# Expert tiles of a graph and mixture-of-experts layer: gathered rows scaled, shifted and split by rows, then turned by transposing DMAs in place of TensorE transposes

## The chip, the cores and the metric

One Trainium2 chip, one core. The metric is the device time of one execution in microseconds (us), the median of several runs. Engines: PE is TensorE, DVE is VectorE, ACT is ScalarE, POOL is GpSimd, SP is SyncE, which here only issues DMAs.

## The reference, cut to what matters

6250 nodes of 256 features pass a graph attention layer and a linear attention layer, which take up the first two thirds of the time and stay as they are. What the change touches is the last layer, a mixture of eight experts of which each node uses two:

```python
logits = xt @ Wr + br                       # xt: the normalized nodes, 6250 x 256
top_p, top_idx = top_k(softmax(logits), 2)
weights = top_p / top_p.sum(-1)
xn = (xt - mu) * rsqrt(var + 1e-5)
xe = xn * ln_g[e] + ln_b[e]                 # scale and shift of expert e, one number per feature
h  = gelu(xe @ W1[e] + b1[e])               # 256 -> 1024
y  = h @ W2[e] + b2[e]                      # 1024 -> 256
out = x + sum over the two experts of weights * y
```

## The kernel before, in words

Until about 1350 us into the span the kernel does the two attention layers, the routing and a sort of the nodes by expert. It ends with a table `places`: for each of FT = 56 tiles of 256 places (two halves of 128, called sub), which node stands in each place, and with `ffn_i`, the expert of each tile. The normalized rows lie in DRAM in `xn2_d` (the trace calls it xn_d).

Each tile s then runs through all engines, with two buffers (u = s % 2) for nearly everything:

- **POOL** (`pool_turn`, L877) makes one turn for each i from 0 to 60, in program order: it waits until a rows buffer is free (`rows_turned`, L880), until the result of tile i - 5 is weighted (`y_gated`) and until both adds of tile i - 6 have landed (`y_added`); it copies the turn's places (`places_now`, L857); issues the first half's indirect add of tile i - 5 into the output in DRAM (`add_rows`, L862); two indirect gathers of weights for tile i - 3 (`get_gates`, L867); waits until the first add has landed; issues the second add (L862); and at last two indirect gathers of 128 rows of 256 float32 for tile i (`get_rows`, L873) into `rows_s[u]`. Turns 0 to 4 add nothing, turns past 55 gather no rows.
- **PE** (`pe_tile`) turns the rows of tile s + 1 with four float32 transposes into PSUM (`pe_turn_rows`, L2219), so that the features lie on the partitions; does 48 matmuls of tile s against W1 (`pe_up`, L2233); and 48 matmuls of tile s - 1 against W2 (`pe_down`, L2253). Values and weights are each split in a high and a low float16 part, three products of them are summed, hence 48.
- **DVE** (`dve_tile`) makes `dve_affine(s + 1)`: two TENSOR_SCALARs read the turned rows from PSUM, multiply and add the expert's scale and shift, which here are one number per partition (L1880, into `x_f`), wait for ACT's high part, and subtract it to get the low part (L1885). Then it splits the activations of tile s (L1900, L1901), four times 512 columns, and forms y of tile s - 1 from PSUM (`dve_answer`, L1914).
- **ACT** (`act_tile`) rounds `x_f` of tile s + 1 to float16 (`act_high`, L1166), makes the gelu of tile s from PSUM (L1145) and weights y of tile s - 1 (`act_gate`, L1158).
- **SP** has nothing to do in this stage: its last DMAs are the weights W2 and the store of the gates (L728), and then it waits for the end (L732).

The scales and shifts of all experts come in at the start with b1 and bq: four small loads on ACT's queue into `param_rows`, one transpose on PE, a copy and a small multiply on DVE (L1277, L1279). Wr and br have a semaphore of their own (`route_in`); POOL waits for the seven other parameter loads before it adjusts a bias (L775, L776).

The order of the stage is fixed by each engine's program order and semaphores:

```python
def pe_tile(b, u):
    s = b * 2 + u
    if not (isinstance(s, int) and s + 1 == FT):
        pe_turn_rows(s + 1, 1 - u, b + u)
    pe_up(s, u)
    ...
        pe_down(s - 1, 1 - u)
```

Of the kernel before, what the change touches and what calls it, by code (L numbers as in the profile page):

```python
# [9 lines left out]
P = 128  # L10
# [26 lines left out]
FR = 2 * P  # L37
# [103 lines left out]
def build(nc, x, src, dst, gnn_w, attn_l, attn_r, gnn_bias, wq, bq, wk, bk, wv, bv, wo, bo,  # L141
          wr, br, ln_g, ln_b, w1, b1, w2, b2, out):
    ctx = ExitStack()
    with ctx:
# [51 lines left out]
        param_rows = first([98, P])  # L196
# [84 lines left out]
        params = sb("params", [P, 98])  # L281
        b1T, gT, bT, bqT = params[:, 0:64], params[:, 64:80], params[:, 80:96], params[:, 96:98]
# [47 lines left out]
        params_s = params[:, 64:96]  # L330
# [28 lines left out]
        x_f = ffn([P, 2, KD, FR])  # L359
# [77 lines left out]
        def high_hots_of(t0, t1):  # L437
# [39 lines left out]
        route_in, blank_turn = sem("route_in"), sem("blank_turn")  # L477
# [22 lines left out]
        place_turn, table_turn, map_turn, places_ready = sem("place_turn"), sem("table_turn"), sem("map_turn"), sem("places_ready")  # L500
        now_ready = sem("now_ready")
        adds_ready, tau_turn = sem("adds_ready"), sem("tau_turn")
        rows_got = [sem(f"rows_got{u}") for u in range(2)]
        gates_got = [sem(f"gates_got{u}") for u in range(2)]
        rows_turned, x_turn, x_high, h_made, gelu_ready, h_turn, y_made, y_ready, y_gated, y_added = (
            sem("rows_turned"), sem("x_turn"), sem("x_high"), sem("h_made"), sem("gelu_ready"), sem("h_turn"),
# [38 lines left out]
        def _(sp):  # L545
# [17 lines left out]
            def load_mix(n):  # L563
                if n < 2:
                    sp.dma_start(w_kv[:, :, n, :], (wk, wv)[n].rearrange("(k p) n -> p k n", p=P)).then_inc(mix_in, 16)
                elif n < 4:
                    sp.dma_start(b_kv[:, n - 2, :], (bk, bv)[n - 2].rearrange("(a n) -> a n", a=1).to_broadcast([P, D])).then_inc(mix_in, 16)
                elif n < 6:
                    sp.dma_start((w_q, w_o)[n - 4][:, :, :], (wq, wo)[n - 4].rearrange("(k p) n -> p k n", p=P)).then_inc(mix_in, 16)
                elif n == 6:  # L570
                    sp.dma_start(bo_b[:, :], bo.rearrange("(a n) -> a n", a=1).to_broadcast([P, D])).then_inc(mix_in, 16)
                elif n == 7:
                    sp.dma_start(wr_s[:, :, :], wr.rearrange("(k p) n -> p k n", p=P)).then_inc(route_in, 16)
                else:
                    sp.dma_start(br_b[:, :], br.rearrange("(a n) -> a n", a=1).to_broadcast([P, X])).then_inc(route_in, 16)
# [150 lines left out]
            load_w2(7)  # L726
            sp.wait_ge(gates_ready, 1)
            sp.dma_start(gate_d.rearrange("(p t) e -> p t e", t=T), gates[:, :, :]).then_inc(gates_out, 16)  # L728

            for g in range(GROUPS - 2, GROUPS):  # L730
                sp.wait_ge(x2_out[g % 2], x2_stored(g))
# [4 lines left out]
        def _(pool):  # L736
# [38 lines left out]
            pool.wait_ge(mix_in, 7 * 16)  # L775
# [142 lines left out]
        def _(act):  # L918
# [3 lines left out]
            act.dma_start(param_rows[64:80, :], ln_g.rearrange("e (f p) -> (e f) p", p=P)).then_inc(params_in, 16)  # L922
            act.dma_start(param_rows[80:96, :], ln_b.rearrange("e (f p) -> (e f) p", p=P)).then_inc(params_in, 16)
            act.dma_start(param_rows[96:98, :], bq.rearrange("(f p) -> f p", p=P)).then_inc(params_in, 16)
# [210 lines left out]
            def act_tile(b, u):  # L1135
                s = b * 2 + u
                if not (isinstance(s, int) and s + 1 == FT):
                    act_high(s + 1, 1 - u)
# [30 lines left out]
            act_high(0, 0)  # L1169
# [12 lines left out]
        def _(dve):  # L1182
# [92 lines left out]
            def keep_params():  # L1275
                dve.wait_ge(params_turned, 1)
                dve.tensor_copy(params[:, :], bank[7][:, 0:98]).then_inc(params_kept, 1)  # L1277
                dve.wait_ge(params_kept, 1)
                dve.tensor_scalar(params_s[:, :], params[:, 64:96], ASCALE, None, ALU.mult).then_inc(params_kept, 1)  # L1279
# [553 lines left out]
            in_turn(dve, map_turn, 0,  # L1833
# [8 lines left out]
            dve.wait_ge(map_turn, 7)  # L1842
# [4 lines left out]
            in_turn(dve, map_turn, 7,  # L1847
# [6 lines left out]
            dve.wait_ge(map_turn, 13)  # L1854
            dve.sem_inc(adds_ready, 1)

            def find_adds():

                dve.wait_ge(unused_placed, 1)
                in_turn(dve, tau_turn, 0,  # L1860
# [9 lines left out]
                dve.wait_ge(tau_turn, 9)  # L1870
# [15 lines left out]

            def dve_tile(b, u):
                s = b * 2 + u
                if not (isinstance(s, int) and s + 1 == FT):
                    e1 = dve.value_load(ffn_i[0:1, bass.ds(s + 1, 1)], min_val=0, max_val=X - 1)  # L1890
                    dve_affine(s + 1, 1 - u, e1)
# [26 lines left out]
            dve.wait_ge(params_kept, 2)  # L1918
            dve.wait_ge(b2_in, 16)
            dve_affine(0, 0, dve.value_load(ffn_i[0:1, 0:1], min_val=0, max_val=X - 1))  # L1920
# [12 lines left out]
        def _(pe):  # L1933
# [7 lines left out]
            def turn_params():  # L1941
                pe.wait_ge(params_in, 4 * 16)
                pe.transpose(bank[7][:, 0:98], param_rows[:, :], ident[0:98, 0:98]).then_inc(params_turned, 1)
# [179 lines left out]
            def keys_hook(b, u):  # L2123
# [4 lines left out]
                if u == 1:  # L2128
                    if not later:
                        pe.wait_ge(mix_in, 7 * 16)  # L2130
# [38 lines left out]
            pe.wait_ge(route_in, 32)  # L2169
# [43 lines left out]
            def pe_turn_rows(s, u, b):  # L2213
                pe.wait_ge(rows_got[u], (b + 1) * 32)
                if not (isinstance(s, int) and s < 2):
                    pe.wait_ge(x_turn, 2 * s - 3)
                for k in range(KD):
                    for sub in range(2):
                        last = pe.transpose(bank[6 + u][:, k * FR + sub * P:k * FR + (sub + 1) * P],  # L2219
                                            rows_s[:, u, sub, k * P:(k + 1) * P], ident[:, :])  # L2220
                last.then_inc(rows_turned, 1)
# [18 lines left out]
            def pe_down(s, u):  # L2240
                if isinstance(s, int) and s == 0:
                    pe.wait_ge(w2_in, X * 16)
                    pe.wait_ge(tau_turn, 1)
# [32 lines left out]
            pe_turn_rows(0, 0, 0)  # L2276
# [37 lines left out]
```

## Time and profile before

| | |
|---|---|
| median of 3 runs | 1996.78 us (1994.44 to 1999.62) |
| the profiled execution, own time | 1998.07 us |
| its span in the profile | 1996.4 us |
| PE busy | 1659.0 us, 83% |
| DVE busy | 1503.7 us, 75% |
| POOL busy | 1325.6 us, 66% |
| ACT busy | 854.8 us, 43% |
| bytes moved by DMA | 238.93 MB, mean 120 GB/s |
| expert stage (first row gather to the end) | about 1357 to 1996 us |

The span is that of one profiled execution; its own time is 1.7 us longer than the span, and 1.3 us above the median. Times of single instructions below are in that span. "Idle before" is what an engine waited just before an instruction, with what released it.

### The profile page before, as it was taken

Reading aid. Unit: us, or ns where it says so; the run is one execution under the profiler, and the core shown is the slowest. Engines: PE = TensorE matmul, PEld = TensorE weight load, DVE = VectorE, ACT = ScalarE, POOL = GpSimd, SP = SyncE. Lnnn points to the kernel's source line nnn. Section 1 sums busy time; section 2 is a strip of 40 time slices with the busy share of each in tenths; the row PEclk is TensorE's granted clock in tenths of the full one; section 3 lists DMA queues with packets and bytes.
Section 4 is the critical chain, followed back from the end, with each engine's and each line's share of the span. In section 5 each row is a group of like instructions: output and inputs, shape, how many; then the busy total and the mean of one; then the engine's idle time right before and its main releaser. Section 6 shows DMA issues by size and latency. Waiting matters only on the chain.

```text
span 1996.4 us, 48372 instructions
## 1 busy us (share of the span) xinstructions
PE 1659.0 (83%) x11492; PEld 1334.3 (67%) x11493; DVE 1503.7 (75%) x4295; ACT 854.8 (43%) x2066; POOL 1325.6 (66%) x1235
## 2 busy tenths in 40 slices
PE   7767777777787788888887675947999999999996
PEld 5545455555556677666765454936888998988885
DVE  6667677878777888888889888988666666666663
ACT  4633344444433444444444443583444434344442
POOL 2077777777777777677767774404777777777774
PEclk8979999999999999999999988557999999999998
DMA  7745556565534554444444553851333333333342
GB/s 218 231 122 144 161 148 172 151 175 159 135 110 113 141 141 128 132 138 135 127 119 131 155 193 106 301 196 35 54 51 46 51 47 52 49 47 51 46 51 28
DMA packets 150531, 238.93 MB, mean 120 GB/s; under 512 B 27984, under 2 KB 116168, under 8 KB 149192
## 3 DMA queue, kind: packets, MB, share of 16 engines
q0 software_dynamic: 62784, 134.26, 30.2%
q1 hardware_dynamic: 85944, 103.15, 15.6%
q10 hardware_dynamic: 1744, 0.85, 0.2%
q8 instruction: 23, 0.38, 0.1%
q14 instruction: 36, 0.29, 0.0%
HBM read 181.73 MB, written 56.44 MB: 119 GB/s over the span
## 4 chain that ended last, share of the span: by engine, by line
PE 31%; issue 19%; DVE 18%; POOL 18%; DVEq 6%; DMA 6%; POOLq 1%; ACT 0%; SPq 0%; ACTq 0%
POOL w_s L805 16%; PE bank L2233 13%; PE bank L2253 13%; DVE w_s L1501 5%; DMA w_s<-table,w_s 3%; DVEq L1436 3%; DMA out<-mid_g,acc 2%; PE bank L2219 1%; DVE w_s L1491 1%; PE bank L2046 1%; DVE w_s L1487 1%; DVE w_s L1484 1%; DMA w_s<-in_x 1%; DVE acc L1512 1%; DVE acc L1664 1%
## 5 line engine op out<-in xcount | busy, mean ns | idle before, releaser
L805 POOL DMA_INDIRECT w_s<-table,w_s x784 | 840.3, 1072 | 281.8 <-issue 235.3
L2046 PE MATMUL bank<-w_s 128*128 128x260 f32 x1952 | 513.3, 409 | 93.7 <-DVE w_s L1501 91.9
L2046 PEld LDWEIGHTS bank<-w_s 128*128 128x128 f32 x1952 | 375.0, 199 | 194.5 <-DVE w_s L1501 118.7
L1501 DVE SCALAR_TENSOR_TENSOR w_s<-w_s 128x256 f32<-128x256 f32 x976 | 347.7, 417 | 0.0
L1001 ACT COPY w_s<-bank 128x512 bf16<-128x512 bf16 x244 | 143.6, 588 | 409.0 <-PE bank L2026 314.3
L2233 PE MATMUL bank<-acc,w_s 128*128 128x256 f16 x2688 | 303.8, 273 | 0.0
L2253 PE MATMUL bank<-w_s,acc 128*128 x2688 | 302.6, 273 | 1.0 <-DVE acc L1914 1.0
L2253 PEld LDWEIGHTS bank<-w_s,acc 128*128 128x128 f16 x2688 | 262.7, 98 | 32.0 <-issue 1.3
L2233 PEld LDWEIGHTS bank<-acc,w_s 128*128 x2688 | 263.4, 98 | 30.8 <-issue 0.2
L862 POOL DMA_INDIRECT out<-mid_g,acc x112 | 196.4, 1753 | 80.7 <-POOL acc L857 47.0
L1468 DVE SCALAR_TENSOR_TENSOR w_s<-w_s,iota 128x512 bf16<-128x512 f32 x244 | 182.9, 749 | 6.7 <-issue 1.4
L1158 ACT ACTIVATE mid_g<-acc 128x256 f32<-128x256 f32 x112 | 50.8, 500 | 304.2 <-DMA out<-mid_g,acc 154.5
L1145 ACT ACTIVATE acc<-bank,params 128x256 f32<-128x256 f32 x448 | 172.7, 480 | 18.7 <-issue 14.8
L1901 DVE SCALAR_TENSOR_TENSOR acc<-acc 128x512 f16<-128x512 f32 x224 | 157.6, 704 | 7.7
L995 ACT ACTIVATE w_s<-w_s 128x16 f32<-128x16 f32 x244 | 56.4, 231 | 233.6 <-DVE w_s L1493 230.3
L989 ACT CAST w_s<-w_s 128x512 f32<-128x512 bf16 x244 | 152.5, 625 | 0.0
L2026 PEld LDWEIGHTS bank<-w_s 128*128 128x128 bf16 x976 | 68.1, 101 | 117.5 <-DVE w_s L1468 69.0
L2036 PE MATMUL bank<-w_s 128*128 x976 | 63.6, 176 | 99.7 <-DVE w_s L1489 51.7
L867 POOL DMA_INDIRECT acc<-gate_d,acc x112 | 117.6, 1050 | 35.2 <-issue 33.6
L2026 PE MATMUL bank<-w_s 128*128 128x128 bf16 x976 | 99.8, 227 | 47.8 <-DVE w_s L1468 46.9
L873 POOL DMA_INDIRECT acc<-xn_d,acc x112 | 111.1, 992 | 35.6 <-issue 26.2
L1914 DVE SCALAR_TENSOR_TENSOR acc<-bank,stage 128x256 f32<-128x256 f32 x112 | 42.3, 419 | 120.2 <-PE bank L2253 120.1
(301 smaller groups left out, 2226.5 us busy)
## 6 DMA issues: line engine op xcount, KB each, us to landing
stage<-in_L_ffn_W SPq DMA_DIRECT2D x32, 512.0 KB, 3.3
w_s<-table,w_s POOLq DMA_INDIRECT x784
w_s<-in_x SPq DMA_DIRECT2D x48, 256.0 KB, 4.2
w_s<-xT_d SPq DMA_DIRECT2D x96, 128.0 KB
w_park<-low_g SPq DMA_DIRECT2D x18, 512.0 KB
w_s<-w_park SPq DMA_DIRECT2D x9, 1024.0 KB, 9.2
xn_d<-acc SPq DMA_DIRECT2D x7, 896.0 KB, 4.7
table<-w_s SPq DMA_DIRECT2D x24, 260.0 KB, 3.6
```

Source lines behind the costliest of these rows:

```text
L805: pool.indirect_dma_start(out=ring[:, u, k, :], out_offset=None, in_=table[:, :], in_offset=bass.IndirectOffsetOnAxis(ap=ids[:, h, at + u, ...
L862: pool.indirect_dma_start(out=out[:, :], out_offset=bass.IndirectOffsetOnAxis(ap=now[:, h, sub:sub + 1], axis=0), in_=gated_s[:, 1 - h, su ...
L989: act.copy(hot32[:, k.at % 4, :, :], hot16[:, k.at % 4, :, :]).then_inc(hot32_ready, 1)
L1001: act.copy(hotT[:, k.at % 2, :, :], turned16).then_inc(hotT_ready, 1)
L1145: last = act.activation(h32[:, f, :], bank[q][:, (f % 2) * FR:(f % 2 + 1) * FR], ACT.Gelu, bias=b1T[:, bass.ds(e * KF + f, 1)], scale=UNSCALE)
L1468: dve.scalar_tensor_tensor(hot16[:, k.at % 4, :, :], dstT[:, bass.ds(group * SUB, SUB)].unsqueeze(2).to_broadcast([P, SUB, P]), tile_v[:, ...
L1501: last = dve.scalar_tensor_tensor(m[:, e:e + GH, 0:GD], rows[:, e:e + GH, 0:GD], 1.0, m[:, e:e + GH, GD:HC].to_broadcast([P, GH, GD]), ALU ...
L1901: lambda: dve.scalar_tensor_tensor(h_hl[:, u, 1, f0:f1, :], h32[:, f0:f1, :], ASCALE, h_hl[:, u, 0, f0:f1, :], ALU.mult, ALU.subtract))
L2026: last = pe.transpose(turned16[:, s, :], hot16[:, k.at % 4, s, :], ident16[:, :])
L2046: last = pe.matmul(bank[2 + k.at % 2][:, 0:ROW], hot32[:, k.at % 4, s, :], msg[:, k.at % 2, s, :], start=s == 0, stop=s == SUB - 1)
L2233: last = pe.matmul(bank[f // 2][:, (f % 2) * FR:(f % 2 + 1) * FR], w1_s[:, bass.ds(e, 1), k, wh, f * P:(f + 1) * P].rearrange("p a b -> p ...
L2253: last = pe.matmul(bank[4 + sub][:, 0:D], h_hl[:, u, hh, f, sub * P:(sub + 1) * P], w2_s[:, bass.ds(e, 1), f // (KF // 2), wh, f % (KF // ...
```

## The change

The scale and shift are applied before the turn, while the rows still lie by nodes: DVE multiplies and adds rows of the expert's scale and shift that SP loads, spread over all partitions, for every tile (`load_affine`); ACT makes the high float16 part by rows (`rows_hl`), DVE the low part by rows in one instruction with the factor 32 folded in. Then SP issues two transposing DMAs per tile (`turn_rows`), each from 128 partitions x 512 float16 (256 high, 256 low) to four blocks of 128 x 128 in `x_hl`. The PE transposes and the semaphore `rows_turned` go; POOL's reuse of a rows buffer now waits for the low part of the tile (`x_turn`). At the start, two of ACT's four small loads go, the multiply L1279 goes, and Wr and br count on the semaphore of the other parameters, so that POOL's L776 waits for nine loads and not seven. Some counters are merged into one.

```diff
+            def load_affine(s, u):
+                e = sp.value_load(ffn_i[0:1, bass.ds(s, 1)], min_val=0, max_val=X - 1)
+                if not (isinstance(s, int) and s < 2):
+                    sp.wait_ge(x_turn, 3 * s - 4)
+                for n, of in enumerate((ln_g, ln_b)):
+                    sp.dma_start(affine[:, u, n, :], of[bass.ds(e, 1), :].to_broadcast([P, D])).then_inc(affine_in[u], 16)
+
+            def turn_rows(s, u):
+                sp.wait_ge(x_turn, 3 * s + 3)
+                if not (isinstance(s, int) and s < 2):
+                    sp.wait_ge(h_made, 4 * s - 4)
+                sp.sem_inc(carried, 1)
+                for sub in range(2):
+                    sp.dma_start_transpose(x_hl[:, u, :, :, sub * P:(sub + 1) * P].rearrange("p h k r -> p (h k) r"),
+                                           rows_hl[:, u, sub, :, :].rearrange("p h d -> p (h d)")).then_inc(xt_in[u], 16)
...
+            for u in range(2):
+                load_affine(u, u)
             sp.wait_ge(gates_ready, 1)
             sp.dma_start(gate_d.rearrange("(p t) e -> p t e", t=T), gates[:, :, :]).then_inc(gates_out, 16)
+            def sp_tile(s, u):
+                turn_rows(s, u)
+                if not (isinstance(s, int) and s + 2 >= FT):
+                    load_affine(s + 2, u)
...
                 if not known_i or i >= 2:
-                    pool.wait_ge(rows_turned, min(i - 1, FT) if known_i else i - 1)
+                    pool.wait_ge(x_turn, min(i - 1, FT) * 3 if known_i else i * 3 - 3)
...
-            def act_high(s, u):
-                act.wait_ge(x_turn, 2 * s + 1)
+            def act_high(s, u, b):
+                act.wait_ge(x_turn, 3 * s + 2)
                 if not (isinstance(s, int) and s < 2):
-                    act.wait_ge(h_made, 4 * s - 4)
-                act.copy(x_hl[:, u, 0, :, :], x_f[:, u, :, :]).then_inc(x_high, 1)
+                    act.wait_ge(xt_in[u], b * 32)
+                act.activation(rows_hl[:, u, :, 0, :], rows_s[:, u, :, :], ACT.Copy, scale=ASCALE).then_inc(x_high, 1)
...
-            def dve_affine(s, u, e):
-                dve.wait_ge(rows_turned, s + 1)
-                if not (isinstance(s, int) and s < 2):
-                    dve.wait_ge(x_high, s - 1)
-                for k in range(KD):
-                    last = dve.tensor_scalar(x_f[:, u, k, :], bank[6 + u][:, k * FR:(k + 1) * FR],
-                                             params_s[:, bass.ds(e * KD + k, 1)], params_s[:, bass.ds(e * KD + k + KD * X, 1)],
-                                             ALU.mult, ALU.add)
-                last.then_inc(x_turn, 1)
+            def dve_affine(s, u, b):
+                def factor(n):
+                    return affine[:, u, n, :].unsqueeze(1).to_broadcast([P, 2, D])
+                dve.wait_ge(rows_got[u], (b + 1) * 32)
+                dve.wait_ge(affine_in[u], (b + 1) * 32)
+                dve.tensor_tensor(rows_s[:, u, :, :], rows_s[:, u, :, :], factor(0), ALU.mult).then_inc(x_turn, 1)
+                dve.wait_ge(x_turn, 3 * s + 1)
+                dve.tensor_tensor(rows_s[:, u, :, :], rows_s[:, u, :, :], factor(1), ALU.add).then_inc(x_turn, 1)
                 dve.wait_ge(x_high, s + 1)
-                dve.tensor_tensor(x_hl[:, u, 1, :, :], x_f[:, u, :, :], x_hl[:, u, 0, :, :], ALU.subtract).then_inc(x_turn, 1)
+                dve.scalar_tensor_tensor(rows_hl[:, u, :, 1, :], rows_s[:, u, :, :], ASCALE, rows_hl[:, u, :, 0, :],
+                                         ALU.mult, ALU.subtract).then_inc(x_turn, 1)
...
-            def pe_up(s, u):
+            def pe_up(s, u, b):
                 e = pe.value_load(ffn_i[0:1, bass.ds(s, 1)], min_val=0, max_val=X - 1)
-                pe.wait_ge(x_turn, 2 * s + 2)
+                pe.wait_ge(xt_in[u], (b + 1) * 32)
...
-                if not (isinstance(s, int) and s + 1 == FT):
-                    pe_turn_rows(s + 1, 1 - u, b + u)
-                pe_up(s, u)
+                pe_up(s, u, b)
```

## Rows read from the trace of the kernel before

**Rows 1.** The page, part 4: the chain that ended last, by engine.
```profile
PE 31%; issue 19%; DVE 18%; POOL 18%; DVEq 6%; DMA 6%; POOLq 1%; ACT 0%; SPq 0%; ACTq 0%
```

**Rows 2.** Busy time by stretch: stretch, length, PE, PEld, DVE, ACT, POOL busy (instructions), PEclk, DMA share, GB/s.
```profile
1400.00:1500.00 100.00, 100.00 (x918) 89.97 (x917) 63.45 (x121) 43.44 (x105) 73.29 (x67) 1.00 0.34 51
```

**Rows 3.** Timeline of PE, one tile: start, us, engine, line, operation, count.
```profile
1700.58 0.60 PE L2219 MATMUL bank<-ident,acc 128*128 128x128 f32 x4
...
1701.02 5.40 PE L2233 MATMUL bank<-acc,w_s 128*128 128x256 f16 x48
...
1706.26 5.40 PE L2253 MATMUL bank<-w_s,acc 128*128 x48
...
1711.50 0.60 PE L2219 MATMUL bank<-ident,acc 128*128 128x128 f32 x4
```

**Rows 4.** Timeline of DVE and ACT between two tiles.
```profile
1711.82 0.76 DVE L1914 SCALAR_TENSOR_TENSOR acc<-bank,stage 128x256 f32<-128x256 f32 x2 [2.14 <-PE bank L2253]
...
1712.89 0.91 ACT L1158 ACTIVATE mid_g<-acc 128x256 f32<-128x256 f32 x2 [5.49 <-DVE acc L1914]
1713.27 1.00 DVE L1880 TENSOR_SCALAR acc<-bank,params 128x256 f32<-128x256 f32 x2 [0.69 <-issue]
...
1714.39 0.62 ACT L1166 CAST acc<-acc 128x512 f16<-128x512 f32 x1 [0.59 <-DVE acc L1880]
1715.04 0.76 DVE L1885 TENSOR_TENSOR acc<-acc 128x512 f16<-128x512 f32 x1 [0.77 <-ACT acc L1166]
```

**Rows 5.** Timeline of POOL, turn copies (L857): the first and last of 46.
```profile
1400.33 0.64 POOL L857 COPY acc<-low_g 128x6 int32<-128x6 int32 x1
...
1888.72 0.18 POOL L857 COPY acc<-low_g 128x6 int32 x1 [0.21 <-ACT mid_g L1158]
```

**Rows 6.** Waits of 1400 to 1900 us: who for whom, us, times, longest.
```profile
POOL acc L857 <- ACT mid_g L1158: 23.4, 37, 1.0
```

**Rows 7.** Timeline of POOL, the two adds of one turn.
```profile
1704.26 1.89 POOL L862 DMA_INDIRECT out<-mid_g,acc  x1 [0.84 <-POOL acc L857]
...
1709.06 2.11 POOL L862 DMA_INDIRECT out<-mid_g,acc  x1 [0.36 <-issue]
```

**Rows 8.** Timeline of the stage's end.
```profile
1962.58 5.40 PE L2233 MATMUL bank<-acc,w_s 128*128 128x256 f16 x48
...
1976.33 1.59 POOL L862 DMA_INDIRECT out<-mid_g,acc  x1 [0.83 <-POOL acc L857]
...
1980.75 1.55 POOL L862 DMA_INDIRECT out<-mid_g,acc  x1 [2.83 <-DMA out<-mid_g,acc]
```

**Rows 9.** Timeline of the stage's start.
```profile
1359.08 0.94 POOL L873 DMA_INDIRECT acc<-xn_d,acc  x1 [0.30 <-issue]
...
1361.92 1.08 PE L2219 MATMUL bank<-ident,acc 128*128 128x128 f32 x4 [9.08 <-DMA acc<-xn_d,acc]
...
1366.09 6.61 PE L2233 MATMUL bank<-acc,w_s 128*128 128x256 f16 x48
...
1388.24 1.00 DVE L1880 TENSOR_SCALAR acc<-bank,params 128x256 f32<-128x256 f32 x2 [0.24 <-issue]
```

**Rows 10.** DMA issues (KB each, us to landing) and queues (packets, MB, share of 16 engines).
```profile
q1 hardware_dynamic: 85944, 103.15, 15.6%
...
xT_d<-w_s SPq DMA_DIRECT2D x48, 128.0 KB, 3.2
...
gate_d<-late SPq DMA_DIRECT2D x1, 196.0 KB, 2.1
```

**Rows 11.** DMA queues between 1400 and 1900 us: packets, MB, share of 16 engines.
```profile
q0 software_dynamic: 20660, 24.66, 32.8%
```

**Rows 12.** Timeline of POOL near the start.
```profile
56.07 1.03 POOL L776 TENSOR_SCALAR w_s<-w_s 128x256 f32<-128x256 f32 x1 [40.59 <-DMA w_s<-in_L_mix_bo]
95.22 0.40 POOL L814 PARTITION_ALL_REDUCE w_s<-w_s  x1 [38.12 <-DVE w_s L1400]
```

**Rows 13.** The last parameter load: duration in ns, start.
```profile
L575 SPq DMA_DIRECT2D br_b<-in_L_ffn_br x1: 542/542/542, 57.0 to 57.0; - x1
```

More of the change, by code:

```diff
@@ L195, in build @@
         edge_rows_f = first([112, 14, P])
-        param_rows = first([98, P])
+        param_rows = first([66, P])
         attn_b = first([P, 2, D])
@@ L280, in build @@
         iota = sb("iota", [P, 256])
-        params = sb("params", [P, 98])
-        b1T, gT, bT, bqT = params[:, 0:64], params[:, 64:80], params[:, 80:96], params[:, 96:98]
+        params = sb("params", [P, 66])
+        b1T, bqT = params[:, 0:64], params[:, 64:66]
         eps_c = sb("eps_c", [P, 1])
@@ L358, in build @@
         rows_s = ffn([P, 2, 2, D])
-        x_f = ffn([P, 2, KD, FR])
+        rows_hl = ffn([P, 2, 2, 2, D], F16)
+        affine = ffn([P, 2, 2, D])
         x_hl = ffn([P, 2, 2, KD, FR], F16)
@@ L499, in build @@
             sem("low_hots"), sem("low_valued"), sem("high_hots"), sem("owners_made"))
-        place_turn, table_turn, map_turn, places_ready = sem("place_turn"), sem("table_turn"), sem("map_turn"), sem("places_ready")
+        place_turn, table_turn, places_ready = sem("place_turn"), sem("table_turn"), sem("places_ready")
         now_ready = sem("now_ready")
-        adds_ready, tau_turn = sem("adds_ready"), sem("tau_turn")
+        adds_ready = sem("adds_ready")
         rows_got = [sem(f"rows_got{u}") for u in range(2)]
         gates_got = [sem(f"gates_got{u}") for u in range(2)]
-        rows_turned, x_turn, x_high, h_made, gelu_ready, h_turn, y_made, y_ready, y_gated, y_added = (
-            sem("rows_turned"), sem("x_turn"), sem("x_high"), sem("h_made"), sem("gelu_ready"), sem("h_turn"),
+        affine_in = [sem(f"affine_in{u}") for u in range(2)]
+        xt_in = [sem(f"xt_in{u}") for u in range(2)]
+        x_turn, x_high, h_made, gelu_ready, h_turn, y_made, y_ready, y_gated, y_added = (
+            sem("x_turn"), sem("x_high"), sem("h_made"), sem("gelu_ready"), sem("h_turn"),
             sem("y_made"), sem("y_ready"), sem("y_gated"), sem("y_added"))
@@ L726, in _ @@
             load_w2(7)
+            def load_affine(s, u):
[12 more added lines that the diff above has]
+                                           rows_hl[:, u, sub, :, :].rearrange("p h d -> p (h d)")).then_inc(xt_in[u], 16)
+            sp.wait_ge(table_turn, 3)
+            sp.wait_ge(owners_made, 1)
+            for g in range(GROUPS - 2, GROUPS):
+                sp.wait_ge(xn2_out[g % 2], stored(g))
+            for u in range(2):
+                load_affine(u, u)
             sp.wait_ge(gates_ready, 1)
             sp.dma_start(gate_d.rearrange("(p t) e -> p t e", t=T), gates[:, :, :]).then_inc(gates_out, 16)
+            def sp_tile(s, u):
+                turn_rows(s, u)
+                if not (isinstance(s, int) and s + 2 >= FT):
+                    load_affine(s + 2, u)
+            for u in range(2):
+                sp_tile(u, u)
+            with sp.Fori(1, FT // 2 - 1) as b:
+                for u in range(2):
+                    sp_tile(b * 2 + u, u)
+            for u in range(2):
+                sp_tile(FT - 2 + u, u)
             for g in range(GROUPS - 2, GROUPS):
@@ L1841, in _ @@
                     lambda: dve.tensor_copy(places[:, 0:FT, 4:6], pairs(mp_w[:, :])))
-            dve.wait_ge(map_turn, 7)
+            dve.wait_ge(table_turn, 10)
             dve.sem_inc(places_ready, 1)
@@ L1846, in _ @@
             dve.sem_inc(gates_ready, 1)
-            in_turn(dve, map_turn, 7,
+            in_turn(dve, table_turn, 10,
                     lambda: dve.tensor_copy(mp_i[:, :], mp_w[:, :]),
@@ L1941, in turn_params @@
             def turn_params():
-                pe.wait_ge(params_in, 4 * 16)
-                pe.transpose(bank[7][:, 0:98], param_rows[:, :], ident[0:98, 0:98]).then_inc(params_turned, 1)
+                pe.wait_ge(params_in, 2 * 16)
+                pe.transpose(bank[7][:, 0:66], param_rows[:, :], ident[0:66, 0:66]).then_inc(params_turned, 1)
             def turn_pair(i, u):
@@ L2129, in keys_hook @@
                     if not later:
-                        pe.wait_ge(mix_in, 7 * 16)
+                        pe.wait_ge(mix_in, 9 * 16)
                     pe_keys(first)
@@ L2166, in _ @@
             walk_turns(pe, pe_slot, keys_hook, keys_hook, queries_hook, None, pe_sum)
-            pe.wait_ge(route_in, 32)
+            pe.wait_ge(mix_in, 9 * 16)
             pe.wait_ge(v_kept, T)
@@ L2211, in _ @@
             last.then_inc(owners_made, 1)
[L2213 to L2221, printed above, removed]
-            def pe_up(s, u):
+            def pe_up(s, u, b):
                 e = pe.value_load(ffn_i[0:1, bass.ds(s, 1)], min_val=0, max_val=X - 1)
-                pe.wait_ge(x_turn, 2 * s + 2)
+                pe.wait_ge(xt_in[u], (b + 1) * 32)
                 for f in range(KF):
```

38 lines of the change are left out of this document (15 added, 23 removed).

## The prediction

> **What bounds the kernel now.** I read the chain that ended last first: PE has the largest share of it, 31% [rows 1], but the chain crosses stages with different limits, and the change acts almost only in the last one. So next comes the busy time by stretch. From 1400 to 1500 us PE is busy for all 100 us, at a granted clock of 1.00 (the 2.4 GHz level), DVE for 63 and POOL for 73 [rows 2]; every stretch up to 1950 looks the same. PE bounds the expert stage without a gap. The timeline shows what a tile costs PE: from one tile's transposes to the next 1711.50 - 1700.58 = 10.92 us, of which 1701.02 to 1706.26 = 5.24 are the W1 matmuls, 1706.26 to 1711.50 = 5.24 the W2 matmuls, and 0.44 the four transposes [rows 3]. Starts are what counts; the 0.60 us duration includes the pipeline's tail.
>
> The second thing to see is how little room POOL has behind PE. 45 POOL turns take 1888.72 - 1400.33 = 488.39 us, 10.85 each [rows 5], and in them POOL waits for a weighted result 23.4 us in all, 0.52 a turn [rows 6]. So a POOL turn is 10.33 us of its own work, though its busy share says 73%: the rest is idle between issues. Inside a turn, the second add waits for the first to land: the first ends its issue at 1704.26 + 1.89 = 1706.15, the second starts at 1709.06, 2.91 us later [rows 7]. At the quiet end of the kernel the same landing takes 1980.75 - (1976.33 + 1.59) = 2.83 us [rows 8]. So that wait has under 0.1 us of cover, the two gathers of weights.
>
> **The change part by part**, against the profiled execution (span 1996.4, own time 1998.07).
>
> *PE transposes removed.* 0.44 us a tile, all of it on the path. 54 tiles (2 to 55) are turned between matmuls: 54 x 0.44 = 23.6 us. Those of tiles 0 and 1 belong to the start. The period falls to 10.48.
>
> *DVE.* It loses the pair L1880 (1.00), the value load before it (most of the 0.69 idle) and L1885 (0.76) [rows 4]; it gains a multiply, an add and a low part, each 128x512, priced as L1885 at 0.76 at most and 0.69 at best: 2.2 us. About as much as before; DVE has 37 us of 100 free [rows 2]. *ACT* rounds the same 128x512 as L1166, 0.62. Neither is on the path.
>
> *When the low part is ready.* Counted from PE's end of a tile: the answer starts 0.32 later and ends at 1.08, the weighting ends at 1713.80 - 1711.50 = 2.3 [rows 3, 4]. Then multiply and add are done by 2.6, ACT's high part by 3.3, the low part by 4.0. Now SP issues the transposes at 4.1, and PE needs them at 10.48: 6.3 us of cover.
>
> *Transposing DMAs added, two of 128 KB a tile.* The trace has none. Lower bound: the store of 196 KB that landed in 2.1 us, plus one more issue, 2.4. Nearest row: two stores of 128 KB issued back to back by SP, 3.2 us each [rows 10], so 3.6 for the pair. Upper bound: a turn of 2-byte elements in pieces of 32 bytes would be 4096 packets a DMA; the hardware queue's packets took 0.156 x 1996 x 16 / 85944 = 0.058 us of an engine each [rows 10], so 4096 x 0.058 / 16 = 14.8 us a DMA, 30 a tile. I take 3.6: the same queue, the same bytes. Cover 6.3, so hidden in the steady state.
>
> What bears on this price is a rule that speaks against the change. The Trainium skill's "VectorE: DVE Perf Modes", section "The three transpose paths", gives 1309 ns for one 128x128 bf16 transpose by the DMA crossbar against 390 ns on TensorE, and advises TensorE where a PSUM destination will do. Eight such blocks a tile would be an estimated 10.5 us in a row where the sum takes 3.6; by it the cover would be gone. The trace shows TensorE's four float32 turns at 0.44 us together, far under that table; it shows nothing of the crossbar.
>
> *Scale and shift loads added, two of 128 KB a tile.* SP issues them a tile and more ahead, each after the add of two tiles before; DVE waits for them only if they land over 10 us late. Nothing on the path. But with the transposes they put 512 KB a tile beside POOL's DMAs, which keep the 16 engines at 32.8% for 24.66 MB in 500 us [rows 11].
>
> *POOL's wait moved, from PE's turn to DVE's low part.* A turn used to start at about 2.5 (after the weighting); now not before 4.1. Queued behind it are the copy, the adds, the weights' gathers and the rows' gather. Alone this shifts POOL by 1.6 us and costs nothing: a gather for tile s + 4 then ends at 4.1 + 10.3 and lands 1361.92 - 1360.02 = 1.9 later [rows 9], at 16.3, and DVE wants it two periods on, at 22.1. What does count is that SP's transposes start on the same semaphore value as POOL's turn, so their bytes run into the first add, whose landing has no cover. Bounds: nothing (the landing was 2.83 us in the quiet and at most 2.91 with the engines a third busy, so load barely shows) up to full serialization: 512 KB at 103.15 MB / 311 us = 331 GB/s [rows 10] is 1.58 us, of which the two landings cover 5.7 of 10.5 us, so 0.85. I take 0.3, nearer the row that saw load: POOL's turn becomes 10.33 + 0.30 = 10.63, above PE's 10.48, and POOL sets the pace.
>
> *Start of the stage.* Before, rows landed at 1361.9 and the first W1 matmul ran at 1366.09 [rows 9]. Now DVE multiplies and adds (1363.4), ACT rounds (1364.1), DVE's low part ends at 1364.9, and the transposes land 3.6 later: 1368.6, so +2.5 (with 2.4 for the pair +1.3).
>
> *Start of the kernel.* POOL's L776 ran at 56.07, the last load that it now awaits is issued at 57.0 [rows 12, 13]; it slips some 6 us, and POOL has nothing to do for the next 38 [rows 12]. Two small loads and one 0.2 us DVE multiply fewer: zero. If that cover were gone, it would cost those 6 us. The order of the gates' store behind four load issues: zero, since SP waited there.
>
> *Sum.* By PE alone: 1996.4 - 23.6 + 2.5 = 1975.3. By POOL: turn 5, the first with adds, waits for tile 3's low part; DVE began that tile at 1388.24 [rows 9], now 2.1 later, plus 2.9 of chain: 1393.2. The turn of tile 55 ends 51 turns later; + 1.9 landing + 2.9 chain + 3.7 transposes, then 1996.4 - 1962.58 = 33.8 from the last W1 block to the end [rows 8]. That is 1435.5 + 51 x P. POOL takes over from PE at P = 10.58; with 10.63 the span is 1977.6. Adding 1.7 gives 1979.3 of own time; the median stands 1.3 below this execution: **1978 us**.
>
> **The rivals.**
>
> *POOL as the bound, dearer* (0.25). The same formula with a collision of 0.4 to 0.85: P = 10.73 to 11.18, so 1983 to 2006, 1991 at the middle. For it: no cover behind the first add, and transposes started by the same event. Against it: the landing hardly differs between a quiet and a third-busy chip. It loses to before from P = 11.0.
>
> *Transposes too late* (0.17), the other side. A pair slower than 6.3 us holds PE before each W1 block. Tile s + 2's low part is ready 4.1 after the end of tile s's W1 and tile s - 1's W2, so two periods are at least 10.5 + 4.1 + D: it decides from D = 6.3, breaks even at 7.3 and costs (14.6 + D)/2 - 10.48 per tile. With packets of 128 bytes, D = 2 x 1024 x 0.058 / 16 + 2.1 = 9.5, the period is 12.05, the time 1975 + 54 x 1.57 = about 2060. The range of D bears this out as possible; the plain stores of the same queue speak against. By the Trainium skill's table (10.5 us a tile) the estimate would be some 2090.
>
> *It does not free PE* (0.02): another wait, such as the scale loads on DVE, keeps 10.9; then 1999.
>
> **How the numbers follow.** Forecast (0.56): PE or POOL at 10.48 to 10.7 a tile, 1973 to 1983, all of it faster by over 0.3% (6 us, about what a measurement of this kernel can tell from no change). Of the 0.25 for the dear POOL, 0.07 is faster, 0.10 the same, 0.08 slower; all 0.17 of the late transposes are counted slower but 0.01, and the last 0.02 is the same. So 0.63 faster, 0.13 same, 0.24 slower. The range runs from 1972 (start +1.3, POOL holding 10.48) to 2015, which takes in the dear POOL and the mildest late transposes, and leaves out their rest, some 0.14.
>
> **What would show it.** PE: W1 block to W1 block 10.48 to 10.7 instead of 10.92, gaps only where POOL's gathers come late, and then DVE's multiply released by a DMA. POOL: L857 without a wait, and more idle before the second add. SP: from the transposes' issue to the first W1 matmul about 3.6 us at the start. It is wrong if PE waits for the transposes at every tile (D over 6.3), or if POOL's turn is over 11.

## The result: slower by 1.0%, and the profile after

The changed kernel takes 2018.01 us (median of 4 runs, 2013.39 to 2020.17) against 1996.67 us of the kernel before (4 runs, 1994.44 to 1999.62): ratio 1.0103, 95% interval 1.0081 to 1.0125. The forecast was 1978 us in a range of 1972 to 2015: wrong in sign, and outside the range. The profiled execution has an own time of 2020.17 and a span of 2018.2 us, 21.8 us more than before.

The page of the changed kernel: busy time, queues (packets, MB, share of 16 engines), the chain that ended last.

```profile
PE 1643.1 (81%) x11268; PEld 1311.1 (65%) x11269; DVE 1521.6 (75%) x4294; ACT 853.7 (42%) x2066; POOL 1325.9 (66%) x1235
...
q0 software_dynamic: 62784, 134.26, 29.9%
q1 hardware_dynamic: 163000, 132.54, 23.5%
...
issue 25%; POOL 23%; DVE 19%; DMA 18%; PE 7%; DVEq 6%; POOLq 1%; ACT 1%; SPq 1%; ACTq 0%
POOL w_s L842 16%; DMA out<-mid_g,acc 9%; DVE w_s L1534 5%; DMA w_s<-table,w_s 5%; POOL acc L910 3%; DMA acc<-xn_d,acc 2%; DVEq L1469 2%; PE bank L2255 2%; PE bank L2275 2%; POOL out L899 2%; POOL acc L904 1%; DVE w_s L1524 1%; DVE w_s L1520 1%; DVE w_s L1517 1%; DVE acc L1697 1%
```

PE's share of the chain has gone from 31% [rows 1] to 7%. "DMA out<-mid_g,acc 9%", the landing of the adds into the output, stands in the chain now: the expert stage has passed from PE to POOL. Queue 1 moves 132.54 MB where it moved 103.15 [rows 10].

Busy time by stretch, same columns as [rows 2].

```profile
1400.00:1500.00 100.00, 100.00 (x918) 89.54 (x917) 69.06 (x125) 45.10 (x109) 72.49 (x64) 1.00 0.62 99
1500.00:1600.00 100.00, 96.08 (x876) 85.00 (x875) 63.22 (x115) 40.86 (x98) 70.09 (x64) 1.00 0.59 94
...
1800.00:1900.00 100.00, 91.85 (x815) 80.57 (x813) 62.37 (x115) 40.47 (x97) 70.37 (x63) 0.97 0.55 91
```

The DMA share is 0.55 to 0.62 where it was 0.34 [rows 2]. PE is full for the first 100 us only, while it uses up its lead, and then has gaps. Its timeline while it is full, from W1 block (L2255) to W1 block:

```profile
1408.68 5.40 PE L2255 MATMUL bank<-acc,w_s 128*128 128x256 f16 x48
1413.92 5.40 PE L2275 MATMUL bank<-w_s,acc 128*128 x48
1419.16 5.40 PE L2255 MATMUL bank<-acc,w_s 128*128 128x256 f16 x48
```

1419.16 - 1408.68 = 10.48 us, against 10.92 before [rows 3]. What PE was to gain, it gained. POOL's timeline, with the adds now at L899 and the copy at L894:

```profile
1446.04 1.69 POOL L899 DMA_INDIRECT out<-mid_g,acc  x1 [0.84 <-POOL acc L894]
...
1451.43 1.62 POOL L899 DMA_INDIRECT out<-mid_g,acc  x1 [1.13 <-issue]
...
1454.65 0.95 POOL L910 DMA_INDIRECT acc<-xn_d,acc  x1 [0.30 <-DVE acc L1918]
1455.61 0.61 POOL L894 COPY acc<-low_g 128x6 int32 x1
1457.05 1.68 POOL L899 DMA_INDIRECT out<-mid_g,acc  x1 [0.83 <-POOL acc L894]
...
1464.16 1.61 POOL L899 DMA_INDIRECT out<-mid_g,acc  x1 [2.67 <-DMA out<-mid_g,acc]
```

Each turn begins the moment the one before ends (1454.65 + 0.95 = 1455.60, copy at 1455.61): the wait before the copy, 0.52 a turn before [rows 6], is 0.24 now. The second add's idle time averages 1.09 us a turn over 50 turns, against 0.50 before; five of them are over 2 us, as at 1464.16. From first add to first add, 50 turns take 562.8 us, **11.26 each**, where before they took 10.86. The whole difference is there: 50 x 0.40 = 20 us, and 2.4 us by which the first add of turn 5 is later (1392.7 after 1390.3); from the first add of turn 55 to the end it is 62.7 after 63.0.

Waits between 1400 and 1960 us (who for whom, us, times, longest):

```profile
DVE acc L1914 <- DMA acc<-xn_d,acc: 49.4, 24, 4.0
...
POOL out L899 <- DMA out<-mid_g,acc: 34.5, 25, 2.8
...
PE bank L2255 <- DMA acc<-acc: 24.8, 14, 4.9
...
POOL acc L894 <- DMA out<-mid_g,acc: 11.9, 12, 2.8
```

PE's wait is put down to the transposes' DMA. The timeline says what kept them late, here for the tile whose W1 block starts at 1707.82 (SPq is the issue by SP):

```profile
1698.35 0.69 DVE L1914 TENSOR_TENSOR acc<-acc 128x512 f32<-128x512 f32 x1 [3.89 <-DMA acc<-xn_d,acc]
...
1700.62 0.72 DVE L1918 SCALAR_TENSOR_TENSOR acc<-acc 128x512 f16<-128x512 f32 x1 [0.78 <-ACT acc L1201]
...
1701.53 2.55 SPq L743 DMA_TRANSPOSE acc<-acc  x2
...
1707.82 7.77 PE L2255 MATMUL bank<-acc,w_s 128*128 128x256 f16 x48 [4.82 <-DMA acc<-acc]
```

DVE's multiply (L1914) was itself waiting for the gathered rows, which POOL issues at the end of its turn. So the chain is POOL's turn, the gather, DVE, the transposes, PE. The same block took 7.77 us where one takes 5.40: behind PE's gap the granted clock was 0.50 (the 1.2 GHz level), as the stretch around it shows, same columns as above:

```profile
1707.00:1712.00 5.00, 4.18 (x20) 3.00 (x21) 2.40 (x5) 2.38 (x5) 3.70 (x3) 0.50 0.42 80
```

This lower clock came behind a gap of PE and is no cause of the loss: POOL sets the pace, and among what POOL waited for from 1400 to 1960 there is no result of PE or ACT.

### The profile page after: what moved, and what is told of

Same layout as the page of the kernel before. It is cut to its first block, busy times and chain, and to the rows that moved or that the text cites. A ratio compares the mean times of both kernels' runs of the same rounds, so it can differ in the third digit from the quotient of the medians.

```text
span 2018.2 us, 48407 instructions
## 1 busy us (share of the span) xinstructions
PE 1643.1 (81%) x11268; PEld 1311.1 (65%) x11269; DVE 1521.6 (75%) x4294; ACT 853.7 (42%) x2066; POOL 1325.9 (66%) x1235
## 3 DMA queue, kind: packets, MB, share of 16 engines
q1 hardware_dynamic: 163000, 132.54, 23.5%
## 4 chain that ended last, share of the span: by engine, by line
issue 25%; POOL 23%; DVE 19%; DMA 18%; PE 7%; DVEq 6%; POOLq 1%; ACT 1%; SPq 1%; ACTq 0%
POOL w_s L842 16%; DMA out<-mid_g,acc 9%; DVE w_s L1534 5%; DMA w_s<-table,w_s 5%; POOL acc L910 3%; DMA acc<-xn_d,acc 2%; DVEq L1469 2%; PE bank L2255 2%; PE bank L2275 2%; POOL out L899 2%; POOL acc L904 1%; DVE w_s L1524 1%; DVE w_s L1520 1%; DVE w_s L1517 1%; DVE acc L1697 1%
## 5 line engine op out<-in xcount | busy, mean ns | idle before, releaser
L2255 PE MATMUL bank<-acc,w_s 128*128 128x256 f16 x2688 | 309.6, 276 | 47.2 <-DMA acc<-acc 46.9
L2255 PEld LDWEIGHTS bank<-acc,w_s 128*128 x2688 | 264.3, 99 | 86.4 <-issue 52.8
L899 POOL DMA_INDIRECT out<-mid_g,acc x112 | 187.6, 1675 | 111.2 <-POOL acc L894 46.9
L910 POOL DMA_INDIRECT acc<-xn_d,acc x112 | 117.8, 1051 | 35.6 <-issue 32.0
L1933 DVE TENSOR_SCALAR acc<-acc 128x512 f16<-128x512 f32 x224 | 103.6, 462 | 34.8 <-ACT acc L1180 34.6
```

The source lines that it names most:

```text
L899: pool.indirect_dma_start(out=out[:, :], out_offset=bass.IndirectOffsetOnAxis(ap=now[:, h, sub:sub + 1], axis=0), in_=gated_s[:, 1 - h, su ...
L910: pool.indirect_dma_start(out=rows_s[:, h, sub, :], out_offset=None, in_=xn2_d[:, :], in_offset=bass.IndirectOffsetOnAxis(ap=now[:, h, 4 + ...
L2255: last = pe.matmul(bank[f // 2][:, (f % 2) * FR:(f % 2 + 1) * FR], w1_s[:, bass.ds(e, 1), k, wh, f * P:(f + 1) * P].rearrange("p a b -> p ...
```

## The experiments

Two theories on what delays POOL. **One-row loads**: the scale and shift loads, 128 packets that all read one row of HBM, delay the landing of POOL's adds. **Transposes**: the transposing DMAs do it, being many small packets, or started together with POOL's turn. The expectations name them by letters: A, any bytes beside POOL's adds delay them; B, the transposes do so beyond their bytes; C, the new DVE and ACT instructions slow POOL; D, it is the one row that makes the loads slow; E, any load of 256 KB at that moment would do. Kernels of one job share a chip and its runs of before. On the chips of the second to fourth jobs the stages ahead of the expert stage take some 300 us longer, in the kernel before too, so ratios are taken within a job only, and across jobs I compare the turn (first add to first add, 50 turns) and the stage (first W1 matmul to the end; before 630.3 us on the first chip, not traced on the others; after 650.4).

| run | ratio to before [95%] | turn us | second add's idle | stage us |
|---|---|---|---|---|
| a1_no_loads | 0.9953 [0.9936, 0.9969] | 10.57 | 0.49 | 616.1 |
| a2_plain_copies | 1.0349 [1.0299, 1.0399] | 11.35 | 0.97 | 655.1 |
| a3_no_transposes | 1.0135 [1.0104, 1.0167] | 11.43 | 0.48 | 658.8 |
| a4_neither | 0.9929 [0.9913, 0.9946] | 10.49 | 0.54 | 611.0 |
| b1_distinct_rows | 0.9980 [0.9939, 1.0021] | 10.70 | 0.54 | 623.7 |
| b2_before_plus_loads | 1.0025 [0.9981, 1.0069] | 10.92 | 1.09 | 634.9 |
| c1_early_copy | 1.0146 [1.0111, 1.0181] | 11.55 | 0.97 | 665.5 |
| c2_spread_rows | 1.0005 [0.9965, 1.0046] | 10.79 | 0.53 | 628.4 |
| d1_after_again | 1.0106 [1.0067, 1.0145] | 11.22 | 0.99 | 650.1 |
| d2_before_plus_loads | 1.0018 [0.9982, 1.0054] | 10.96 | 1.10 | 633.3 |
| d3_spread_rows | 1.0007 [0.9969, 1.0045] | 10.75 | 0.65 | 626.7 |
| d4_spread_early | 1.0159 [1.0092, 1.0227] | 11.21 | 0.50 | 650.7 |
| e1_spread_rows | 1.0005 [0.9967, 1.0044] | 10.62 | 0.47 | 618.3 |
| e2_spread_early | 1.0110 [1.0072, 1.0149] | 11.01 | 0.52 | 637.9 |
| e3_early_copy | 1.0068 [1.0032, 1.0104] | 11.16 | 1.32 | 644.3 |

**First job: take away one part at a time.** a1 loads scale and shift for tiles 0 and 1 only; every later tile uses those of an earlier one (DVE's wait for them goes with them).

```diff
                 turn_rows(s, u)
-                if not (isinstance(s, int) and s + 2 >= FT):
-                    load_affine(s + 2, u)
```

> Leaves out the scale and shift loads after the first two tiles (the multiply and add use stale rows), transposes stay. Theory A (any extra DMA work beside POOL's adds stretches their landing, and the serial chain of POOL's turn, 11.26 us in the changed kernel against 10.33 before, passes it on): about half of the extra goes, turn near 10.8, time 1990 to 2000. Theory B (the crossbar transposes disturb far beyond their bytes): turn stays near 11.2, time above 2010. Theory C (the new row-wise DVE instructions slow POOL's issue): no change, 2018.

a2 keeps everything but turns no rows: its two DMAs copy the same bytes plainly, so the matmuls get unturned rows.

```diff
-                    sp.dma_start_transpose(x_hl[...], rows_hl[...])
+                    sp.dma_start(x_hl[...], rows_hl[...])
```

> Each transposing DMA becomes a plain SBUF-to-SBUF DMA of the same 128 KB (x_hl then isn't turned). Theory A, bytes count: turn stays at 11.0 to 11.3, time 2008 to 2018. Theory B: turn falls to about 10.8, time 1990. Theory C: 2018. If a late landing of the transposes themselves held PE, the start of the stage and PE's gaps shrink here.

a3 leaves the transposes out from tile 2 on (the matmuls read the first tiles' rows again), and a4 leaves out both.

```diff
+                if isinstance(s, int) and s < 2:
                     for sub in range(2):
                         sp.dma_start_transpose(...)
+                else:
+                    sp.sem_inc(xt_in[u], 32)
```

> Leaves out the transposing DMAs after the first two tiles: SP raises the semaphore by itself, PE reads a stale x_hl; loads stay. Theory A: the other half goes, turn near 10.8, time 1988 to 1998. Theory B: nearly all goes, turn 10.4, time about 1978. Theory C: PE-side latency gone, turn still 11.2, time 2010 or more.

> Leaves out both, after the first two tiles: neither transposing DMAs nor scale and shift loads; DVE's and ACT's new instructions stay. Theories A and B: turn back to about 10.3, PE sets the pace at 10.48 a tile, time 1974 to 1980. Theory C: turn stays over 10.9, time above 2000.

Before's median here was 1995.66 us; a1 took 1987.11, a2 2060.33, a3 2026.05, a4 1981.73. Without the loads the change is **faster** than before; without the transposes it is at least as slow as with them. The four kernels with and without each part stand like this by POOL's turn: neither 10.49, transposes alone 10.57, loads alone 11.43, both 11.26. So theories A and B fall, which had the turn fall in a3 (to 10.8 and 10.4), and C falls with a4, which keeps all new DVE and ACT instructions. The queues from 1400 to 1900 us (packets, MB, share of 16 engines) of a1, with transposes alone on q1:

```profile
q0 software_dynamic: 21251, 25.17, 35.5%
q1 hardware_dynamic: 51136, 12.33, 12.0%
```

and of a3, with loads alone:

```profile
q0 software_dynamic: 19680, 23.44, 27.8%
q1 hardware_dynamic: 12672, 11.54, 15.2%
```

For about the same bytes the one-row loads hold the engines longer, with a quarter of the packets: 0.152 x 500 x 16 / 12672 = 96 ns for a packet of the loads, 0.120 x 500 x 16 / 51136 = 18.8 ns for one of the transposes. Both averages include the 4-byte packets that go with each DMA; a load packet of 1 KB alone took 106 ns on average in a3's records of packets. PE, in a1, is full again (same columns as the stretches above):

```profile
1400.00:1500.00 100.00, 100.00 (x919) 89.63 (x917) 66.82 (x123) 42.26 (x102) 74.93 (x67) 1.00 0.46 73
...
1800.00:1900.00 100.00, 99.93 (x917) 89.32 (x915) 68.27 (x122) 43.61 (x105) 76.58 (x67) 1.00 0.46 73
```

In a3 the wait has another place. Its waits and one turn (adds at L902, copy at L897):

```profile
POOL acc L897 <- DMA out<-mid_g,acc: 43.1, 37, 2.5
```

```profile
1501.59 1.62 POOL L902 DMA_INDIRECT out<-mid_g,acc  x1 [0.30 <-issue]
1503.52 1.00 POOL L913 DMA_INDIRECT acc<-xn_d,acc  x1 [0.30 <-issue]
1504.83 0.95 POOL L913 DMA_INDIRECT acc<-xn_d,acc  x1 [0.30 <-issue]
1506.33 0.18 POOL L897 COPY acc<-low_g 128x6 int32 x1 [0.55 <-DMA out<-mid_g,acc]
```

With no 2.5 us of transposes' issue ahead of them, SP's loads go out at the low part and meet the second add (half of their packets start 6.1 to 8.2 us into the turn, the second add at 4.8), which then lands later than the two row gathers behind it can hide. The copy waits 1.02 us a turn for it. So the loads cost wherever they meet an add. a4 gives PE its bound back: 100.00 busy in every stretch looked at, stage 611.0 where the prediction's PE alone gives 1975.3 - 1368.6 = 606.7. In a2 the plain copies cost no less than the transposes: in the profiled execution (2024.11 us, ratio 1.014) the turn is 11.35. Its other three took 31 to 53 us longer, and the 1.0349 in the table comes from them; they were not traced, and what slowed them is open.

**Second job: is it the one row, and does it take the rest of the change?** b1 loads as many bytes in as many packets from 128 different rows; scale and shift are then not the expert's. b2 is the kernel before with the one-row loads added, which nobody waits for.

```diff
-                for n, of in enumerate((ln_g, ln_b)):
-                    sp.dma_start(affine[:, u, n, :], of[bass.ds(e, 1), :].to_broadcast([P, D]))...
+                for n in range(2):
+                    sp.dma_start(affine[:, u, n, :], xn2_d[bass.ds(e * P, P), :])...
```

> The scale and shift loads read 128 different rows of 1 KB (of the stored nodes) in place of one row 128 times; same bytes, same moments, other values in the multiply and add. Theory D (all 16 engines reading one row of HBM is what is slow: 96 ns of an engine a packet against 19 for the transposes): packets fall to 50 to 60 ns, POOL's turn to 10.6 to 10.8, time 1985 to 1998. Theory E (any 256 KB load started by the low part hits the second add): turn stays 11.2, time 2010 to 2020.

> The kernel before, with nothing changed but SP loading scale and shift rows for each tile into a spare buffer when the tile's low part is ready. Nobody waits for them. Theory A/D/E (the loads stretch the adds' landing and with it POOL's turn): POOL loses its 0.5 us of wait a turn and passes 10.92, turn 11.2 to 11.4, time 2010 to 2020. If the loads hurt only together with the changed kernel's other waits: no change, 1996.

b1's turn is 10.70, the second add's idle 0.54. Its q1 and b2's, each over 1750 to 2200 us:

```profile
q1 hardware_dynamic: 58546, 22.25, 21.0%
```

```profile
q1 hardware_dynamic: 11919, 10.85, 13.2%
```

b2's packets took 0.132 x 450 x 16 / 11919 = 80 ns. Of b1's 0.210 x 450 x 16 = 1512 us of engines, 47538 packets of transposes at a1's 18.8 ns are 894; 618 are left for 86 x 128 = 11008 load packets, an estimated 56 ns. By size in the records of packets, one of 1 KB took 89 ns on average in b2 and 55 in b1, so the estimate holds. The average hides the shape: in both kernels half of these packets took 46 ns or less, but 18% of b2's were over 150 ns, against 3% of b1's. From the first to the last of a tile's 256 load packets it took 3.9 us in the changed kernel, 3.8 in b2 and 1.6 in b1. Same bytes, same count, other rows: over a third less engine time, and next to no delay of the adds (second add's idle 0.54, turn 0.13 over a1's). b1's rows also lie in another tensor, which was not varied by itself. b2 shows the opposite half: with nothing of the change but the loads, the second add's idle goes from 0.50 to 1.09 and the wait before the copy from 0.51 to 0. The turn is 10.92: the loads use up all of POOL's slack, and the time, ruled by PE at 10.92, hardly moves (1.0025, an interval that holds 1). The expectation of a turn of 11.2 to 11.4 and 2010 to 2020 us missed that: the slack of 0.5 took nearly all of the delay. The kernel before hid this cost; the change takes PE to 10.48 and uncovers it.

**Second to fourth job: a repair, and a second theory.** c2, d3 and e1 are one kernel, which leaves nothing out: once, early, SP writes scale and shift 128 times over into HBM, and each tile loads 128 rows of 2 KB from there, with one DMA in place of two.

```diff
-                for n, of in enumerate((ln_g, ln_b)):
-                    sp.dma_start(affine[:, u, n, :], of[bass.ds(e, 1), :].to_broadcast([P, D]))...
+                sp.dma_start(affine[:, u, :, :], spread_d[bass.ds(e, 1), :, :, :]...)
```

c1 and e3 are the changed kernel with POOL's copy for turn i + 1 put behind turn i's first add (four buffers, loop unrolled by four). It tests the theory that what binds POOL is its own serial issue, of which the copy and the 0.83 us between it and the first add could be saved. d4 and e2 are both together.

```diff
                     add_rows(h, v, 0)
+                    places_next(i + 1, w)
                     get_gates(h, v)
```

> The changed kernel, but POOL copies the places of turn i + 1 inside turn i (four buffers), so that the copy and its 0.83 us to the first issue leave the serial chain add, landing, add, landing. Correct output. Theory A (that chain is the bound): turn down by 0.8 to 1.0 to 10.3 to 10.5, time 1975 to 1990, faster than before. If PE or DVE held the pace in the changed kernel: unchanged, 2018.

> The changed kernel with a correct form of the distinct rows: the scales and shifts are spread once over 128 rows in DRAM, and each tile loads 128 different rows of 2 KB with one DMA in place of two. Theory D: as the kernel without loads or a little over it, turn 10.6, time 1985 to 1995. Theory E: 2010 to 2020.

> The changed kernel once more, beside the next three on one chip: a POOL turn of 11.2 to 11.6 us, 1 to 1.5% slower than before.

> The kernel before with the one-row loads for each tile, which nobody waits for. In the first run POOL's turn was 10.92, without any wait left. Theory D: between PE-bound and POOL-bound, 1996 to 2008, second add's idle time about 1.0 us instead of 0.5. If the loads are harmless by themselves: 1996, idle time 0.5.

> Changed kernel with the scales and shifts spread over 128 rows in DRAM. Theory D: turn 10.7 to 10.8, time 1985 to 2000, 1 to 1.5% faster than the changed kernel. Theory E: as the changed kernel.

> Spread rows and the early copy of the places together. If POOL's chain is what is left once the one-row loads are gone, its own turn falls to 9.8 to 10.2, POOL waits again, PE sets the pace at 10.48 a tile: time 1975 to 1985, faster than before and than the changed kernel. If the early copy is what made the earlier kernel with it slow: 2000 or more.

> Changed kernel with the scales and shifts spread over 128 rows in DRAM, once more, beside the next two. On a chip where before takes 1996 us: the two earlier runs of it had the expert stage (first W1 block to the end) at 627 and 628 us against 650 of the changed kernel and 630 of before, so 1988 to 1998.

> Spread rows and the early copy of the places. If the slow result with the early copy (stage 651 us) came from stalls of all engines that those chips showed also in the stages before: now 1978 to 1988, stage 612 to 618, POOL's turn at PE's 10.5. If the early copy itself is harmful (a landing that comes later because the adds are issued earlier, into the transposes): 2000 or more again, with the add's idle time where the copy was.

> Early copy with the one-row loads. If the serial chain of adds and landings is the bound of the changed kernel: 1985 to 2005, clearly under its 2018. If the early copy itself is harmful: 2018 or more.

d1 repeats the result on another chip (1.0106, turn 11.22), d2 repeats b2. Spread rows bring the turn to 10.62 to 10.79 and the stage to 618.3 to 628.4, against 650.1 of the changed kernel (d1); beside it in the same job, d3's ratio is 1.0007 where d1's is 1.0106. It does not come out below 1 (e1: 1.0005, interval 0.9967 to 1.0044, which leaves room for a gain of 0.3%); against a before of 1996 us, c2 (expected at 1985 to 1995) just missed its range, and d3 and e1 are at the upper end of theirs. By the stage alone e1 should be some 12 us ahead of before; where its walk and its one-time write spend that is open, as before's stage on those chips was not traced.

The early copy fell as a theory. c1 and d4 were slower, not faster, and d4's second add idles only 0.50. Its timeline shows why it is no judge of the copy:

```profile
1935.62 0.13 PEld L2266 LDWEIGHTS bank<-acc,w_s 128*128 x2 [0.59 <-issue]
...
1936.36 0.38 PE L2266 MATMUL bank<-acc,w_s 128*128 128x256 f16 x2 [0.45 <-issue]
...
1937.39 0.27 PE L2266 MATMUL bank<-acc,w_s 128*128 128x256 f16 x1 [0.65 <-issue]
...
1939.04 2.30 ACT L1191 ACTIVATE acc<-bank,params 128x256 f32<-128x256 f32 x6 [4.15 <-remote]
...
1940.00 0.43 DVE L1944 TENSOR_SCALAR acc<-acc 128x512 f16<-128x512 f32 x1 [4.39 <-issue]
```

PE breaks up inside a block with nothing to wait for, and ACT and DVE stand still with it. Such gaps (matmuls over 0.4 us apart inside a block) add up to 26.7 us in d4, 25.8 in c1 and 19.4 in e2, against 1.9 in the changed kernel and in e1, 3.7 in e3. b1, c2 and d3, whose loop is not unrolled, have 7 to 9 us of them, which may be why c2 and d3 stand at 10.75 and more and e1 at 10.62. So e3 is the only fair sight of the early copy, and there the turn was 11.16 and the stage 644.3 with one-row loads: 6 us below d1's, of another job, so at best a small gain, where with spread rows (e2, d4) the copy's move went with a longer stage. The unrolled loop alone does not bring the gaps: c1 and e3 are one kernel, with 25.8 and 3.7. What does was not tried.

## Why the prediction was wrong

**Right.** PE's period (10.48 as forecast). DVE's and ACT's cost: multiply, add and low part take 0.69 each (priced 0.69 to 0.76), ACT 0.63 (priced 0.62). The chain: PE's tile ended at 1419.16 and in the same turn

```profile
1422.43 0.69 DVE L1918 SCALAR_TENSOR_TENSOR acc<-acc 128x512 f16<-128x512 f32 x1 [0.79 <-ACT acc L1201]
...
1423.32 2.52 SPq L743 DMA_TRANSPOSE acc<-acc  x2
```

the low part was done 3.96 us later (forecast 4.0) and the transposes were issued at 4.16 (forecast 4.1). POOL sets the pace, its turns no longer wait for a weighted result, and the second add's idle grows, as the text said they would show.

**The transposes' price** was mis-sized, with little harm. At the stage's start:

```profile
1362.12 0.69 DVE L1918 SCALAR_TENSOR_TENSOR acc<-acc 128x512 f16<-128x512 f32 x1 [0.75 <-ACT acc L1201]
...
1362.92 2.64 SPq L743 DMA_TRANSPOSE acc<-acc  x2
...
1367.78 1.46 PE L2255 MATMUL bank<-acc,w_s 128*128 128x256 f16 x6 [19.42 <-DMA acc<-acc]
```

From issue to the first W1 matmul is 1367.78 - 1362.92 = 4.9 us for the pair, where I took 3.6: each transposing DMA holds SP's queue 1.26 us (median of 112) where I had back-to-back stores in mind. 4.9 is under the cover of 6.3. Beside the loads it was more at times, 1707.82 - 1701.53 = 6.3 for the tile shown above, but all of PE's waits at W1 blocks come to 24.8 us between 1400 and 1960, and POOL waited for none of them: the rival *transposes too late* did not come about. The Trainium skill's "VectorE: DVE Perf Modes", "The three transpose paths", would have made it an estimated 10.5 us; the trace does not bear out adding up its 1309 ns block by block. "Advanced Engine Details and Errata", "X-Bar Transpose (TRN2)", says that transpose DMAs are as fast as regular ones. Packet by packet the trace agrees: one of 256 bytes took 18.5 ns of an engine in a2's plain copies and 19.6 in the changed kernel's transposes. From issue to use it does not; a2 at the start of the stage, where the same bytes are copied plainly:

```profile
1363.93 1.35 SPq L743 DMA_DIRECT2D acc<-acc  x2
...
1367.07 2.31 PE L2255 MATMUL bank<-acc,w_s 128*128 128x256 f16 x10 [17.02 <-DMA acc<-acc]
```

That is 3.1 us for the pair of copies, 1.35 of them issue, against 4.9 and 2.64 for the pair of transposes.

**The step that failed** is "Scale and shift loads added ... Nothing on the path", with the collision that I took at 0.3 and bounded at 0.85. It measured 11.26 - 10.33 = 0.93. I priced all 512 KB alike, by bytes, at 331 GB/s, the mean rate of that queue over the whole kernel. But the transposes' bytes cost POOL's turn next to nothing (a1 at 10.57 against a4 at 10.49, where PE's pace may hide a little more), and the one-row loads' bytes much (0.69 on top of a1, 0.94 on top of a4): two of them take 256 x 106 ns / 16 = 1.7 us of all engines where 256 KB at that rate is 0.8, and they run into the adds. That the loads' source was one row for all 128 partitions stood in the diff, and I had no row of the trace for such a load and gave it no bound of its own. The turn became 11.26 where I took 10.63, above my upper bound of 11.18. This was the rival *POOL as the bound, dearer*, dearer still than its dearest.

**A second failure** is the end of the sum. I let the end follow from the last W1 block, 33.8 us after it. But at the end of turn 55 POOL still has turns 56 to 60, five turns with adds, before it, and the last W1 block is no measure of them. Turn 5 starts at 1392.7 - 1.1 = 1391.6, 51 turns of 11.26 end at 1965.9, and the end comes 52.3 later, not 42.3: from the last W1 block to the end it is now 2018.2 - 1977.64 = 40.6 us:

```profile
1977.64 5.40 PE L2255 MATMUL bank<-acc,w_s 128*128 128x256 f16 x48
```

POOL's turns ended the kernel before as well (the 63.0 and 62.7 above), and they were in its trace. Put together: 1977.6 + 51 x 0.63 + 10.0 - 1.6 = 2018.1, the measured span being 2018.2. With this end, my own 10.63 would have given 1391.6 + 51 x 10.63 + 52.3 = 1986, a gain of 0.5% and not 1%; a1, at 10.57, has a span of 1988.6 (its first add of turn 5 comes 4.6 us later).

The break-even was off with it: the turn must stay below 10.8, not 11.0, for the change to gain. b1, at 10.70, stands at 0.998, with an interval that holds 1.

## What to carry to other kernels

Price an added DMA by its source as well as by its bytes: a broadcast of one HBM row to 128 partitions, small as it is, delayed the accumulating DMAs beside it, and 128 distinct rows hardly did. Before taking work from the engine that bounds a stage, add up the next engine's turn with every wait in it that has no cover: here the second engine was 0.5 us behind and one DMA's landing was bare. And follow the end of the sum along the engine that will set the pace, with all that it still has to do after the last tile.

## What the runs showed of the hardware

- A load of one 1 KB row into 128 partitions took 89 to 106 ns of an engine a packet on average (b2, a3), 55 with 128 different rows (b1). Half of the packets were no slower in b2 than in b1, at 46 ns or less; 18% were over 150 ns, against 3%. Two such loads took 3.8 to 3.9 us from first to last packet, against 1.6. Why one row is slower is not shown.
- Two transposing DMAs of 128 KB (SBUF to SBUF) took 4.9 us from issue to use, 2.6 of them SP's issue, where two plain copies of the same bytes took 3.1 and 1.35; with 544 packets each at 18.8 ns (51136 in 94 of them, a1) they lengthened POOL's turn by 0.08 us (a1 against a4) when they ran beside it alone.
- In three of the four runs with POOL's loop unrolled by four (d4, c1, e2, not e3), PE, ACT and DVE stood still together now and then, ACT and DVE for over 4 us at a time, and PE for 19 to 27 us in sum. The cause is open.
- Behind a gap of 4.82 us before a W1 block, TensorE's granted clock was 0.50 (1.2 GHz) from 1707 to 1712 us, and the block took 7.77 us instead of 5.40.
